# Weighting two of eight value heads on GpSimd instead of VectorE, in the first six blocks of the second layer

## The reference

```python
kv = jax.nn.silu(jnp.einsum('btd,ed->bte', x, W_kv).reshape(b, t, h, d, 2))
k, v = (kv[..., 0], kv[..., 1])
s = jnp.einsum('hd,bthd->bth', q_proj, k)
m_A = jax.lax.cummax(s, axis=1)
exp_scores = jnp.exp(s - m_A)
u_A = jnp.cumsum(exp_scores, axis=1)
w_A = jnp.cumsum(exp_scores[..., None] * v, axis=1)
output = (w_A / u_A[..., None]).mean(axis=2)
...
t = t + _L1_attn_ref(_ln_t(t), ...)
t = t + _L1_ffn_ref(_ln_t(t), ...)
```

## Time and profile before

| what | value |
|---|---|
| median of 3 runs | 2660.29 us (2659.02 to 2660.37) |
| the profiled execution | 2660.01 us, span 2658.3 us |
| PE busy | 2526.1 us |
| VectorE busy | 2183.8 us |
| GpSimd busy | 2032.9 us |
| ScalarE busy | 1854.1 us |
| scans L1471 | 256, together 286.8 us for the 224 with a carry |
| weighings L1463 | 256, 174.6 us, 682 ns each |

### The profile page before, as it was taken

One profiled execution on the slowest core, in us unless ns is written; L12 is line 12 of the kernel. 1 busy time (PEld: TensorE's weight loads), 2 busy tenths in 40 slices (PEclk: granted clock), 3 DMA queues, 4 the chain that ended last, 5 costly groups with the idle time before them and its releaser, 6 DMA issues.

```text
span 2658.3 us, 36321 instructions
## 1 busy us (share of the span) xinstructions
PE 2526.1 (95%) x10665; PEld 1835.9 (69%) x10665; DVE 2183.8 (82%) x3276; ACT 1854.1 (70%) x3414; POOL 2032.9 (76%) x1500
## 2 busy tenths in 40 slices
PE   6999999999999999999999999998888999999878
PEld 4888877788887778888778878875445555555443
DVE  6788887788888778888788888873699888988995
ACT  5677777677777767677776667776887777777650
POOL 4787877778887777887678877875458989888883
PEclk9999999999999999999999999999999999999999
DMA  1000000010000010000000100101435666475555
GB/s 68 5 13 9 9 13 9 9 44 9 9 15 11 9 40 9 13 13 9 9 9 9 37 13 9 40 21 54 151 132 220 229 235 229 177 261 208 214 200 215
DMA packets 58102, 198.35 MB, mean 75 GB/s; under 512 B 12752, under 2 KB 15376, under 8 KB 40496
## 3 DMA queue, kind: packets, MB, share of 16 engines
q1 hardware_dynamic: 57904, 196.03, 20.8%
HBM read 178.04 MB, written 17.96 MB: 74 GB/s over the span
## 4 chain that ended last, share of the span: by engine, by line
PE 48%; POOL 26%; issue 14%; DVE 6%; ACT 4%; DMA 1%; POOLq 0%; SPq 0%; DVEq 0%; ACTq 0%
POOL p_lo L220 23%; PE m_ps L358 5%; PE om_ps L387 5%; PE s_ps L373 5%; PE om_ps L389 5%; PE om_ps L388 5%; PE s_ps L375 5%; PE s_ps L374 5%; PE mo_ps L1272 4%; DVE v_ps L1463 1%; PE k_ps L1228 1%; DVE ay L1471 1%; PE row_ps L1252 1%; PE v_ps L1228 1%; PE k_ps L1229 1%
## 5 line engine op out<-in xcount | busy, mean ns | idle before, releaser
L220 POOL TENSOR_TENSOR p_lo<-pf,p_hi 128x512 fp32r<-128x512 f32 x1024 | 1319.5, 1293 | 390.6 <-ACT p_hi L510 387.9
L505 ACT ACTIVATE pf<-s_ps 128x512 f32<-128x512 f32 x1024 | 613.1, 599 | 508.2 <-PE s_ps L375 506.6
L649 DVE TENSOR_REDUCE mx<-m_ps 128x1 f32<-128x512 f32 x1024 | 701.8, 687 | 254.9 <-PE m_ps L358 248.2
L665 DVE TENSOR_TENSOR sum_ps<-sum_ps,pf 128x512 f32<-128x512 f32 x960 | 662.5, 690 | 20.0 <-ACT pf L505 19.6
L510 ACT CAST p_hi<-pf 128x512 fp32r<-128x512 f32 x1024 | 627.3, 613 | 0.0
L373 PE MATMUL s_ps<-q_hi,kd_hi 128*128 128x512 f32 x1024 | 424.9, 415 | 0.0
L358 PE MATMUL m_ps<-w_both,q_hi 128*128 128x512 f32 x1024 | 405.2, 397 | 7.6 <-DVE mx L649 6.5
L387 PE MATMUL om_ps<-p_hi,v_hi 128*128 128x512 f32 x1024 | 402.1, 393 | 6.2 <-POOL p_lo L220 6.2
L375 PE MATMUL s_ps<-q_lo,kd_hi 128*128 128x512 f32 x1024 | 400.1, 391 | 0.0
L374 PE MATMUL s_ps<-q_hi,kd_lo 128*128 128x512 f32 x1024 | 400.0, 391 | 0.0
L388 PE MATMUL om_ps<-p_hi,v_lo 128*128 128x512 f32 x1024 | 399.4, 390 | 0.0
(11 more groups left out here) (226 smaller groups left out, 3596.5 us busy)
## 6 DMA issues: line engine op xcount, KB each, us to landing
bq<-weight_rows SPq DMA_DIRECT2D x64, 1024.0 KB, 6.6
gate_b<-gate_rows SPq DMA_DIRECT2D x60, 1024.0 KB, 4.8
xb<-in_x_dram SPq DMA_DIRECT2D x8, 1024.0 KB, 6.1
rb_sb<-inverse_rows SPq DMA_DIRECT2D x32, 256.0 KB, 3.9
tokens<-xb SPq DMA_DIRECT2D x32, 256.0 KB, 2.0
tp<-tokens SPq DMA_DIRECT2D x32, 256.0 KB, 5.4
rb<-norm_rows SPq DMA_DIRECT2D x32, 256.0 KB, 5.4
tv<-tokens SPq DMA_DIRECT2D x32, 256.0 KB, 6.2
```

The source lines that it names most:

```text
L220: nc.gpsimd.tensor_tensor(p_lo[:, r, :], pf[:, r, :], p_hi[:, r, :].bitcast(F32), ALU.subtract).then_inc(lo_done, 1)
L505: nc.scalar.activation(pf[:, g % RING, :], s_ps[:, g % 2, :], ACT.Exp, scale=SCALE).then_inc(exp_done, 1)
L649: nc.vector.tensor_reduce(mx[:, n % 2, sub, chunk:chunk + 1], m_ps[:, j % 2, :], AX.X, ALU.max).then_inc(m_max, 1)
L665: nc.vector.tensor_tensor(sum_ps[:], sum_ps[:], p, ALU.add).then_inc(sum_done, 1)
```

## The change

In the blocks v = 0 to 5 the heads 2 and 6 (`ASIDE`) go another way. ScalarE writes their silu into a quarter of the tile xg in SBUF and not over the PSUM bank. GpSimd multiplies it by w there (`weighed`). VectorE leaves out the weighing of these heads and scans them from xg. The four quarters serve two blocks; ScalarE waits for the scan of two blocks before. The first gated product on GpSimd waits until all scans of the six blocks are done, since it overwrites xg. The count of weighings that other waits go by is kept by the weighing of head 3 or 7, which counts two.

```diff
+    ASIDE = (2, 6)
...
+        def aside(v, h):
+            return v < F_LAG - V_LAG and h in ASIDE
+        def aside_count(v, h):
+            return len(ASIDE) * v + ASIDE.index(h) + 1
+        def aside_slot(v, h):
+            n = aside_count(v, h) - 1
+            return xg[:, n % 4 // 2, n % 2, :]
...
+                if f == 0 and p == 0:
+                    pool.wait_ge(y_dve, (F_LAG - V_LAG) * HEADS)
                 nc.gpsimd.tensor_tensor(xg[:, p % 2, :, :], gate_pair(f, p), twice(tv[:, f % NV, :]), ALU.mult).then_inc(xg_pool, 1)
+
+            def weighed(v, h):
+                q = 2 * v + h // HALF
+                pool.wait_ge(b_in[q % 3], 16 * (q // 3 + 1))
+                pool.wait_ge(v_act, v * HEADS + h + 1)
+                z = aside_slot(v, h)
+                nc.gpsimd.tensor_tensor(z, bq[:, q % 3, h % HALF, :], z, ALU.mult).then_inc(z_pool, 1)
...
                     if stage(v - 1) and h == 0:
                         add_heads(v - 1, 3)
+                    if stage(v) and h == 0 and aside(v, ASIDE[0]):
+                        weighed(v, ASIDE[0])
+                    if stage(v - 1) and h == 0:
                         carried(v - 1, 1)
                         add_halves(v - 1)
...
+                    if stage(v) and h == 6 and aside(v, ASIDE[1]):
+                        weighed(v, ASIDE[1])
                     if stage(v) and h == 7:
                         add_heads(v, 2)
...
+                if aside(v, h):
+                    after(act, y_dve, (v - 4 // len(ASIDE)) * HEADS + h + 1)
+                    nc.scalar.activation(aside_slot(v, h), value_bank(v, h), ACT.Silu).then_inc(v_act, 1)
+                    return
...
-                nc.vector.tensor_tensor(zv, bq[:, q % 3, h % HALF, :], zv, ALU.mult).then_inc(z_dve, 1)
+                both_done = 2 if h and aside(v, h - 1) else 1
+                nc.vector.tensor_tensor(zv, bq[:, q % 3, h % HALF, :], zv, ALU.mult).then_inc(z_dve, both_done)
...
-                dve.wait_ge(z_dve, v * HEADS + h + 1)
+                if aside(v, h):
+                    dve.wait_ge(z_pool, aside_count(v, h))
+                else:
+                    dve.wait_ge(z_dve, v * HEADS + h + 1)
...
-                nc.vector.tensor_tensor_scan(ay[:, h, :], ay[:, h, :], value_bank(v, h),
+                nc.vector.tensor_tensor_scan(ay[:, h, :], ay[:, h, :],
+                                             aside_slot(v, h) if aside(v, h) else value_bank(v, h),
...
-                    if stage(v):
+                    if stage(v) and not aside(v, h):
                         weigh(v, h)
```

More of the change, by code:

```diff
@@ L913, in scan_attention_and_experts @@
         clr = sem("clr")
+        z_pool = sem("z_pool")
         def after(eng, s, count):
```

## The result

The changed kernel takes 2671.03 us in the median of five executions, against 2660.33 for the one before on the same chip: +10.7 us, ratio 1.0038, 95% interval 1.0028 to 1.0049, so it is slower by 0.4%, clear of the noise. A sixth execution fell into a slower state of the chip (4854.66 us); such executions are left out of all medians here. The forecast was 2670.0, with a range of 2661.5 to 2672.5. The profiled execution took 2669.39 us, with a span of 2667.7.

A forecast was written before the change was run, and what follows sets the result against it. VectorE was taken to set the pace of the six blocks. With GpSimd first, 2.4 + 3.0 + 1.7 + 3.0 + 1.0 - 1.4 = +9.7 us on 2660.3 gave 2670.0, range 2661.5 to 2672.5.

The forecast's parts named there:

- VectorE sets the pace, GpSimd has time at the wrong moments: Blocks 0 to 5: VectorE busy 106.12 of 117.00 us, GpSimd 62.69, but GpSimd is occupied when products are needed.
- S + 5.10: Predicted end of head 6's GpSimd product, 5.10 us after head 3's scan ends; VectorE, ready at 3.60, waits 1.5 us.
- A scan with two SBUF inputs is held by GpSimd: Scans of heads 2 and 6: a held 1.22 us scan ends 1.09 us after the GpSimd instruction.
- The tie goes to GpSimd: When one end releases both engines, GpSimd goes first: head 6's scan ends 3.0 us later; total +9.7 us, chance 0.45.
- VectorE first: Rival: VectorE is served first when both engines are released together; +3.2 us, 2663.5 us, chance 0.26.
- Block by block: Costs with GpSimd served first: block 1 2.4 + 3.0, block 2 1.7 + 3.0, block 4 1.0, block 5 -1.4 us.
- +1.0 in either case: Block 4, head 2: the residual ends at 1969.1 in place of 1968.1, whichever engine is served first.
- The difference stays until the end: Behind 2003 us no wait is tied to a fixed time, so the whole difference reaches the end.
- offload pays: Rival: scans with two SBUF inputs are not held; -1.6 us, 2658.7, or full gain 2651.8; chance 0.08.

The follow-up runs named there:

- both ties turned: Changed kernel with GpSimd's carry copy moved between head 6's product and the next add, plus a small copy between halves and xf: 2663.83 us, +4.3 us.
- head 2 alone: Against the kernel before: only head 2 of blocks 0 to 5 goes through GpSimd, head 6 stays on VectorE; 2663.65 us, +3.1 us.
- block 5 alone: Against the kernel before: heads 2 and 6 go through GpSimd in block 5 only; 2659.13 us, -0.7 us, not told from nothing.
- waits alone: Changed kernel with all products and waits kept, but scans of heads 2 and 6 read the PSUM bank; 2663.24 us, +2.7 us against the kernel before.
- both kernels with a moved copy: Changed kernel with GpSimd's carry copy between head 6's product and the next add: 2665.74 us; the same plus a small copy behind the halves: 2663.83 us.
- the kernel with eight pairs: Against the kernel before: eight GpSimd products placed where GpSimd is idle, head 2 of blocks 0, 4, 5 and head 4 of blocks 1 to 5; 2656.81 us, -2.8 us.

## Why the prediction was right

- *VectorE sets the pace, GpSimd has time at the wrong moments:* right. The waits ahead of head 6 are 1.41 to 1.44 us in blocks 0 to 2 (1.32 in block 4) where 1.5 was worked out from S + 5.10.
- *A scan with two SBUF inputs is held by GpSimd:* right, and shown by itself: 2.95 against 1.22 us with the source of one operand changed.
- *The tie goes to GpSimd:* this was the choice between +9.7 and +3.2 us, and it was argued from two start times 0.1 us apart, not from a row that showed it. It came out so at the scans of head 6 and at the residuals, and moving a copy turned it round. That the choice was right is in part luck: the traces now have places where, at 0.05 us, one or the other goes first. With both ties turned the loss is 4.3 us; the forecast for VectorE first was +3.2.
- *Block by block:* within 0.1 us up to block 4. Block 4 cost 1.5 us in place of 1.0: VectorE waits 0.37 us for ScalarE ahead of head 1, which no term had. With head 2 alone block 4 cost nothing, so that the term "+1.0 in either case" was too firm: the loss reaches block 5 only if head 6 has used up the slack.
- *The difference stays until the end:* right only roughly. With the first block's 0.26 us counted in, the start of block 6 is +10.5, the end of block 31 +11.8 and the span +9.4. The last 2.4 us came back in the tail: 1.6 in two waits for gate rows (3.30 and 0.49 us after, 4.10 and 1.30 before) and most of the rest in the wait for TensorE behind them (0.42 against 1.29). The prediction had neither the rise nor the fall; that they leave the traces 0.3 us from the forecast of +9.7 is luck. A gain does not stay, as block 5 alone shows: 1.2 of its 1.5 us are gone by block 9.
- *The rival "offload pays":* it fell as it was put (+2.7 us even with the scans free of holding, where -1.6 was its price), since the residual is held too: 1.77 and 1.78 us for those of blocks 0 and 1 in the kernel with waits alone. With other heads it is true.

## What to carry to other kernels

Before work goes to a less busy engine, write down when that engine is free against the moment at which the result is needed; its share of idle time says nothing of it, and what is queued behind the new instruction moves as well. When an operand moves from PSUM to SBUF and the other one is there already, GpSimd can hold VectorE's instruction (here for up to 2.2 us), so look at what GpSimd starts at that moment. The instruction that is new on GpSimd can in turn hold others of VectorE with two SBUF inputs, which were never touched. Where the two engines are released together, an instruction of 0.2 us between them can decide who pays.

## What the runs showed of the hardware

- A GpSimd instruction and a VectorE instruction with two SBUF inputs, released by the same end: GpSimd's starts 0.07 us ahead and goes first (scan 3.37 us). With a copy of 0.19 us between, VectorE's scan without a carry starts 0.06 us ahead and goes first (1.23 us), and the GpSimd add behind it takes 3.36 us in place of 2.37.
- The start in the trace is not by itself the order of service. A scan with a carry that starts 0.06 us ahead of the add loses in block 4 of both kernels with a moved copy; one that starts 0.05 us ahead of a product wins in block 5 of the kernel with eight pairs. With 0.16 us ahead every scan won, with a carry or without.
- A held scan of 1.22 us ends 1.07 us after the GpSimd instruction's recorded end, a held residual of 0.67 us 0.55 us after it. By these two differences the recorded end is 0.12 to 0.15 us later than the moment at which VectorE gets through (an estimate).
- The Trainium skill, "SBUF — State Buffer", section "Who interferes with whom", has it that whoever issues first keeps the shared ports and the other is blocked. The runs agree, but for the scans of block 4, where the start in the trace and the order of service differ; the measurement decides there.
